# Turning the quantized attention weights of a cross-attention with transposing DMA transfers instead of TensorE and ScalarE

## The reference

```python
q, k = _fq_sym(q, axis=-1), _fq_sym(k, axis=-1)     # rounded to -127..127 times a scale
v = _fq_sym(v, axis=2)
attn = jnp.einsum('bhqd,bhkd->bhqk', q, k)          # 16 heads, 2048 x 2048
attn = jax.nn.softmax(attn.astype(jnp.float32), axis=-1)
attn = _fq_unsigned(attn, axis=-1)                  # round(attn / s), 0..255, s = row max / 255
out = jnp.einsum('bhqk,bhkd->bhqd', attn, v)
```

## Time and profile before

| What | Value |
|---|---|
| Time, median of 2 runs | 3344.57 us (3343.7 to 3345.44) |
| The profiled execution's own time | 3347.38 us |
| Its span in the trace | 3345.4 us |
| TensorE busy | 2880.7 us, 86% |
| VectorE busy | 2028.1 us, 61% |
| ScalarE busy | 1721.9 us, 51% |
| GpSimd busy | 331.7 us, 10% |

### The profile page before, as it was taken

How to read it: one execution, slowest core, us unless ns; L and a number is a source line. 1 busy time by engine, 2 the same in 40 slices (tenths; PEclk the granted TensorE clock), 3 DMA queues, 4 the chain that set the end, 5 groups by cost and what they waited for, 6 DMA issues and landing times. The chain is left out here.

```text
span 3345.4 us, 61561 instructions
## 1 busy us (share of the span) xinstructions
PE 2880.7 (86%) x20564; PEld 1826.3 (55%) x20564; DVE 2028.1 (61%) x4452; ACT 1721.9 (51%) x2944; POOL 331.7 (10%) x358
## 2 busy tenths in 40 slices
PE   4999999999766888888888699799948879999998
PEld 2677777777533555555555355455525545555554
DVE  3677777777468999999999512366626632323222
ACT  1565556555445999999999111365615521111110
POOL 0121221211320000000000100111112300000000
PEclk9999999999888999999999599899969979999999
DMA  4000000000000000000000100000050000000000
GB/s 163 1 0 0 0 0 0 0 0 0 11 17 7 0 0 0 0 0 0 0 0 0 41 0 0 13 0 0 0 152 11 9 1 0 0 0 0 0 0 25
DMA packets 34294, 38.13 MB, mean 11 GB/s; under 512 B 2948, under 2 KB 32448, under 8 KB 33216
## 3 DMA queue, kind: packets, MB, share of 16 engines
q10 hardware_dynamic: 17360, 19.22, 1.8%
q1 hardware_dynamic: 16880, 18.19, 1.7%
HBM read 35.29 MB, written 2.10 MB: 11 GB/s over the span
## 5 line engine op out<-in xcount | busy, mean ns | idle before, releaser
L2310 DVE TENSOR_TENSOR f_h<-f_act_g,f_p_u 128x512 f32<-128x512 f32 (+1 forms) x132 | 90.7, 687 | 547.8 <-PE f_p_y L2205 480.4
L1325 PE MATMUL x_p_s<-x_kT,x_qz 128*128 128x512 bf16 x1024 | 303.6, 386 | 99.7 <-DVE f_wg L1407 66.5
L2255 ACT ACTIVATE f_act_g<-f_p_g 128x512 f32<-128x512 f32 (+1 forms) x132 | 78.4, 597 | 576.5 <-PE f_p_g L2190 571.4
L1407 DVE TENSOR_SCALAR_CACHE_REDUCE f_wg<-x_p_s,x_nsq 128x1024 f32<-128x1024 f32 x256 | 318.5, 1281 | 51.7 <-issue 48.4
L1407 DVE TENSOR_SCALAR_CACHE_REDUCE f_wu<-x_p_s,x_nsq 128x1024 f32<-128x1024 f32 x256 | 327.4, 1279 | 12.2
L1334 PEld LDWEIGHTS x_p_t<-identb,x_ints 128*128 128x128 bf16 x4096 | 240.9, 98 | 86.3 <-ACT x_turned L1393 44.7
L2190 PE MATMUL f_p_g<-f_xT,f_wg 128*128 128x512 f32 (+1 forms) x528 | 270.9, 637 | 15.4 <-ACT f_xT L2242 10.1
L1384 ACT ACTIVATE x_ints<-f_wg,x_nb 128x2048 uint16<-128x2048 f32 x128 | 256.3, 2002 | 43.0 <-DVE x_nb L1424 43.0
L1334 PE MATMUL x_p_t<-identb,x_ints 128*128 128x128 bf16 x4096 | 273.0, 220 | 4.1 <-ACT x_turned L1393 4.0
L1384 ACT ACTIVATE x_ints<-f_wu,x_nb 128x2048 uint16<-128x2048 f32 x128 | 256.2, 2002 | 0.6 <-DVE x_nb L1424 0.6
L1393 ACT COPY x_turned<-x_p_t 128x1024 int32<-128x1024 int32 x256 | 254.3, 993 | 2.3 <-PE x_p_t L1334 2.3
(11 more groups left out here) (351 smaller groups left out, 5289.6 us busy)
## 6 DMA issues: line engine op xcount, KB each, us to landing
f_wg<-in_L_ffn_w_dram ACTq DMA_DIRECT2D x2, 1408.0 KB, 10.8
f_wu<-in_L_ffn_w_dram ACTq DMA_DIRECT2D x2, 1408.0 KB, 10.8
f_wd<-in_L_ffn_w_dram ACTq DMA_DIRECT2D x1, 2816.0 KB, 11.0
x_res<-in_x_dram SPq DMA_DIRECT2D x1, 2048.0 KB, 9.0
a_wq<-in_L_attn_Wq_dram ACTq DMA_DIRECT2D x1, 2048.0 KB, 7.7
a_wk<-in_L_attn_Wlk_dram ACTq DMA_DIRECT2D x1, 2048.0 KB, 12.1
a_wv<-in_L_attn_Wlv_dram ACTq DMA_DIRECT2D x1, 2048.0 KB, 16.3
a_wo<-in_L_attn_Wo_dram ACTq DMA_DIRECT2D x1, 2048.0 KB, 22.0
```

Of the source, the lines that this page charges most:

```text
L1325: mm = pe.matmul(p_s[half][:, c * BANK:(c + 1) * BANK], qz[:, par, :, :, :].rearrange("p a b t -> p (a b) t")[:, bass.ds(n, 1), :].rearran ...
L1407: dve.tensor_scalar(score[par][:, half, :], p_s[half][:, :], of_pass(nsq[:, par, :, :].rearrange("p a b -> p (a b)"), n), HIGHEST, ALU.mul ...
L2255: act.activation(act_g[n % 2][0:m, :], p_g[n % 2][0:m, :], ACT.Silu).then_inc(gate_up.sem, 1)
L2310: i = dve.tensor_tensor(h[n % 2][0:m, :], act_g[n % 2][0:m, :], p_u[n % 2][0:m, :], ALU.mult)
```

## The change

TensorE's `turn` (step 4) and ScalarE's `leave` (step 5) are taken out. In their place SyncE issues, for each pass and head, one DMA transfer from the SBUF buffer `ints[par]` to the SBUF buffer `turned[par]` with `transpose=True`: 128 rows of 2048 16-bit integers, 512 KB, that come out as 16 blocks of 128 x 128, each turned. SyncE waits for `exps` of the same pass (`e_up`) and for `values` of the pass before (`o_made`), in this order, with an increment of a semaphore that nobody waits for (`seen`) behind each wait, and then issues. The transfer raises `t_read[par]`, now one semaphore for each head with 16 increments for each transfer. `values` waits for it, and so does `exps` of the next pass, which writes `ints[par]` again. The PSUM tile `x_p_t` stays allocated, without use. VectorE's program is as it was.

```diff
--- before.py
+++ after.py
@@ -1309,13 +1309,14 @@
         s_made, s_read = count("s_made", 4), count("s_read", 4)
         bias_up = count("bias_up", 2)
         e_up = count("e_up", 2)
-        t_made, t_read = count("t_made", 2), count("t_read", 2)
+        t_read = [count(f"t_read{par}", 16) for par in range(2)]
+        seen = sem("x2_seen")
         o_made, o_read = count("o_made", 2), count("o_read", 1)
         block = ctx.enter_context(nc.Block())
 
         @block.tensor
         def _(pe):
-            for c in (s_made, t_made, o_made):
+            for c in (s_made, o_made):
                 c.open(pe)
 
             def scores(a, n, par, half):
@@ -1327,17 +1328,10 @@
                                    kT[:, a, at:at + BANK], start=True, stop=True)
                 mm.then_inc(s_made.sem, 1)
 
-            def turn(a, n, par):
-                pe.wait_ge(e_up.sem, e_up.of(n, par + 1))
-                pe.wait_ge(t_read.sem, t_read.of(n, 1) if par else t_read.of(n - 1))
-                for k in range(B):
-                    mm = pe.transpose(p_t[:, k * P:(k + 1) * P], ints[par][:, k, :].bitcast(BF16), core.identb[:, :])
-                mm.then_inc(t_made.sem, 1)
-
             def values(a, n, par):
                 if not par:
                     pe.wait_ge(o_read.sem, o_read.of(n - 1))
-                pe.wait_ge(t_read.sem, t_read.of(n, par + 1))
+                pe.wait_ge(t_read[par].sem, t_read[par].of(n))
                 for k in range(B):
                     mm = pe.matmul(p_o[:, par * XD:(par + 1) * XD], turned[par][:, k, :].bitcast(F16),
                                    vi[:, k, (2 * a + par) * XD:(2 * a + par + 1) * XD], start=(k == 0), stop=(k == B - 1))
@@ -1351,8 +1345,6 @@
                     if here:
                         scores(*here, 0)
                         scores(*here, 1)
-                    if earlier:
-                        turn(*earlier)
                     if oldest:
                         values(*oldest)
 
@@ -1374,28 +1366,34 @@
 
         @block.scalar
         def _(act):
-            for c in (e_up, t_read):
-                c.open(act)
+            e_up.open(act)
 
             def exps(par):
                 def run(n):
                     act.wait_ge(bias_up.sem, bias_up.of(n, par + 1))
-                    act.wait_ge(t_made.sem, t_made.of(n - 1, par + 1))
+                    act.wait_ge(t_read[par].sem, t_read[par].of(n - 1))
                     act.activation(ints[par][:, :, :].rearrange("p k n -> p (k n)"), score[par][:, :, :].rearrange("p s n -> p (s n)"),
                                    ACT.Exp, bias=nb[:, par:par + 1], scale=-1.0,
                                    accum_out=of_pass(esum[:, :, :, par].rearrange("p a b -> p (a b)"), n)).then_inc(e_up.sem, 1)
                 return run
 
-            def leave(par):
+            pipeline(act, [("exp0", 0), ("exp1", 0)], {"exp0": exps(0), "exp1": exps(1)}, PASSES)
+
+        @block.sync
+        def _(sp):
+            for c in t_read:
+                c.open(sp)
+
+            def turn(par):
                 def run(n):
-                    act.wait_ge(t_made.sem, t_made.of(n, par + 1))
-                    act.wait_ge(o_made.sem, o_made.of(n - 1, par + 1))
-                    act.copy(turned[par][:, :, :].rearrange("p k n -> p (k n)").bitcast(I32),
-                             p_t[:, :].bitcast(I32)).then_inc(t_read.sem, 1)
-                return run
-
-            pipeline(act, [("exp0", 0), ("leave1", 1), ("exp1", 0), ("leave0", 0)],
-                     {"exp0": exps(0), "leave1": leave(1), "exp1": exps(1), "leave0": leave(0)}, PASSES)
+                    sp.wait_ge(e_up.sem, e_up.of(n, par + 1))
+                    sp.sem_inc(seen, 1)
+                    sp.wait_ge(o_made.sem, o_made.of(n - 1, par + 1))
+                    sp.sem_inc(seen, 1)
+                    sp.dma_start(turned[par][:, :, :], ints[par][:, :, :].rearrange("p k n -> p (k n)"), transpose=True).then_inc(t_read[par].sem, 16)
+                return run
+
+            pipeline(sp, [("turn0", 0), ("turn1", 0)], {"turn0": turn(0), "turn1": turn(1)}, PASSES)
 
         @block.vector
         def _(dve):
```

## The result

The changed kernel takes 3388.92 us (median of 2 runs) against 3344.57 us: 44 us more, a ratio of 1.0131 with a 95% interval of 1.0104 to 1.0157.

What follows compares the result with a forecast made beforehand. VectorE was taken to bound the stage at 6.07 us a pass; exponential and handovers 2.4 plus transfer 4.8 give 7.2, so (7.2 - 6.07) x 128 = 145 us, plus 1 for the drain: 3490 us, range 3412 to 3592, whole 3338 to 4335.

Steps and rivals of the forecast that it cites:

- What bounds the kernel before: In the one changed stage, VectorE sets the 6.07 us pass, with ScalarE 0.19 us behind; VectorE's 0.39 us gap is its own.
- The loop through `ints`: One buffer per head: a pass cannot be shorter than exponential 2.1, handover 0.1, transfer 4.8 and handover 0.2 us.
- L, which no row shows: Time from a transfer's issue to its landing: taken as 4.8 us, between 3.1 and 8.5; hidden up to 3.67.
- The term T: Moving time of one 512 KB transposing transfer on the DMA engines: taken as 3.2 us, between 1.5 and 6.9.
- The upper end: Highest moving time of a transfer: 2048 pieces of 256 bytes at 54 ns over 16 DMA engines, 6.9 us.
- the forecast: Transfer not hidden in the changed stage: pass 7.2 us, 3490 us in all, range 3412 to 3592, chance 0.40.
- P: Length of one pass of the changed stage: the larger of 6.07 and 2.4 + L, taken as 7.2 us.
- The handover to SyncE: From the exponential's end to SyncE's issue, over two waits and two increments: 0.1 us, between 0 and 0.6.
- The rival "hidden": Transfer hidden behind the pass, P at most 6.6 us: 3345 to 3412 us, most likely 3350; chance 0.32.
- the signs on record: Profile after: for the forecast, ScalarE waits for DMA, VectorE for ScalarE, landing 4.8 us; if hidden, ScalarE waits on `x_nb`.
- The clock: TensorE's clock in the stage: cost taken as 0; rival has 1.2 GHz, pass up to 7.6 us, 3540, chance 0.03.
- The queue as the bound: Rival: the pass's two transfers share DMA engines or SyncE, pass 8.0 to 13.8 us, 3590 to 4335; chance 0.21.

Runs made afterwards that it cites:

- both new limits away: Changed kernel with two `ints` buffers for each head and 32 unused TensorE transposes a pass put back: 1.0004 of the kernel before.
- the halves: Changed kernel with each transfer issued as two of 8 blocks: 1.0269 of the kernel before, a pass of 6.70 us.
- the filler: Changed kernel with TensorE's 32 transposes a pass put back, turning identity into the unused PSUM tile, nobody waiting: 1.017 of the kernel before.

## Why the prediction was off

*What bounds the kernel before:* right. VectorE bounds it, and its 0.39 us gap is its loop edge, since unrolling the loop takes nearly half of it away. That the removed copies and transposes are worth nothing by themselves: right; ScalarE's busy time fell by a third and no time came of it, and with both new limits away the pass is 6.07 us, as before.

*The loop through `ints`:* right as a mechanism. It is the limit of the changed kernel (link by link 6.47 us, and 6.44 by the period), and two buffers cut it.

*The step that failed is "L, which no row shows".* The term T was mis-sized: I took 3.2 us of moving, the geometric middle of 1.5 and 6.9, and it is 1.8, by the halves and by the 287 GB/s while a transfer moves. The upper end priced a piece of 256 bytes like a packet of 1.1 KB, at 54 ns. The number of pieces was right, 2048 a transfer; by the queue's line above a packet of 256 bytes takes 72.6% x 16 x 700 / 451217 = 18 ns, and at a share of 1.26 the 128 packets of an engine are through in 1.8 us. The fixed part was taken at 1.6 and is 1.9, and 0.2 come on top in the changed kernel. So L is 3.9, not 4.8: T alone was off by 1.4 us, and the smaller errors took 0.5 of it back. The rule that the prediction weighed, 261 GB/s from the Trainium skill's page "DMA: Bandwidth & Descriptors", section "Latency and other measured facts", comes nearest, with 2.0 us. The page gives it for a middle dimension that is not contiguous, and 350 to 400 GB/s for the contiguous case; here both buffers are contiguous in each row, and the engines moved 287. The 1309 ns for a block, from its page "VectorE: DVE Perf Modes", section "The three transpose paths", is no price for each of many: here a further block costs 0.11 us. Since only what exceeds 3.67 us of L counts, an error of 0.9 us in L took away most of the forecast: by its own formula P = 2.4 + 3.9 = 6.3, 29 us. A threshold near the estimate makes the forecast far less certain than the term.

*The handover to SyncE:* mis-sized the other way, 0.1 taken and 0.28 measured, +23 us. With both terms put right the working gives 6.47 us and 51 us, against 44 to 47 measured.

*The rival "hidden"* had the right time (3345 to 3412), and its condition held, T at most 2.6. But the transfer is not hidden: the exponential waits 2.39 us for it, and of the signs on record those of the forecast came, not those of the rival. The forecast had the mechanism and missed the size.

*The clock:* I took 0 and named a rival. The clock did fall, to 1.2 GHz for nearly the whole stage, where I had thought that the work left room; and it cost 0 in the changed kernel, because a pass of 6.44 us covers it. Behind the first limit it was the next one, 6.29 us, as soon as the loop was cut. I had bounded it by TensorE's total work, 5.2 to 7.5 us; it was 5.0 (four pairs at 0.94 and two sets of values at 0.6), and it bit in the one chain from `keep` to the first scores. (The 7.6 in the rival's text should be the 7.5 of its own sum.)

*The queue as the bound:* not here, as 2T is 3.6 us of a 6.44 us pass, and not with the load doubled either.

## What to carry to other kernels

Work taken from an engine that waits for another is worth nothing until the other is relieved: the same transfers that cost 1.3% alone are part of a version that is 2% faster, once `ints` has two buffers, TensorE's order has no wait ahead of the scores, and VectorE does less. When a copy between engines becomes a transfer, give its source a second buffer at once; with a single buffer a pass cannot be shorter than the round trip of exponential, handovers and 3.9 us of transfer. And look at what the removed work did besides: here TensorE's transposes held its clock up.

## What the runs showed of the hardware

A transposing transfer from SBUF to SBUF of 128 x 2048 two-byte elements landed 3.7 us after its issue (3.9 in the changed kernel, where the two of a pass are issued 2.0 us apart) and one of 128 x 1024 after 2.8: 1.9 us fixed and 0.11 us for each 128 x 128 block. It moved in packets of 256 bytes, 18 ns each, at 279 and 287 GB/s in the two stretches read. Together, two a pass, the transfers left VectorE, ScalarE and TensorE at their old pace (6.07 us a pass with a DMA share of 0.78). The issue holds the queue's engine for 1.64 us and 1.23 us, where a plain transfer held it 0.46. TensorE's granted clock was 1.00 with 32 transposes in each pass, useful or not, and 0.50 without them; TensorE was busy 542.70 us of 700 by the records with the filler, at 2.4 GHz, and 495.13 without, at 1.2 GHz.
